# Second attention: the causal mask taken from TensorE products to a minimum on VectorE

## What is computed

```python
scores = jnp.einsum('bhqd,bhkd->bhqk', q, k) / jnp.sqrt(jnp.asarray(d_k, x.dtype))
causal = jnp.tril(jnp.ones((t, t), dtype=bool))
scores = jnp.where(causal, scores, jnp.asarray(-jnp.inf, scores.dtype))
attn = jax.nn.softmax(scores, axis=-1)
y = jnp.einsum('bhqk,bhkd->bhqd', attn, v)
```

## Time and profile before

| | us |
|---|---|
| three runs | 711.42, 712.61, 714.70 (median 712.61) |
| the profiled execution | 712.78 |
| its span, first to last instruction | 711.0 |
| PE busy | 636.5 (90%) |
| DVE busy | 450.6 (63%) |
| ACT busy | 324.3 (46%) |
| POOL busy | 120.9 (17%) |

### The profile page before, as it was taken

One profiled execution on the slowest core, in us unless ns is written; L12 is line 12 of the kernel. 1 busy time (PEld: TensorE's weight loads), 2 busy tenths in 40 slices (PEclk: granted clock), 3 DMA queues, 4 the chain that ended last, 5 costly groups with the idle time before them and its releaser, 6 DMA issues.

```text
span 711.0 us, 11162 instructions
## 1 busy us (share of the span) xinstructions
PE 636.5 (90%) x4151; PEld 393.0 (55%) x4204; DVE 450.6 (63%) x1270; ACT 324.3 (46%) x548; POOL 120.9 (17%) x117
## 2 busy tenths in 40 slices
PE   6877665576999999999999999999999999999897
PEld 2755223363567667666666666555565655554443
DVE  4687658426575775775775776765857576665364
ACT  2477456314555655655655655344433534352110
POOL 2130001132133133132122222011020200000000
PEclk9987987678999999999999999999999999999899
DMA  9300000299965974975894791909166290000000
GB/s 345 169 0 1 0 0 15 50 119 132 120 105 75 99 109 80 87 116 84 74 121 79 69 130 42 97 21 117 13 100 50 61 89 16 1 16 1 16 0 30
DMA packets 83261, 50.64 MB, mean 71 GB/s; under 512 B 4052, under 2 KB 82644, under 8 KB 82900
## 3 DMA queue, kind: packets, MB, share of 16 engines
q1 hardware_dynamic: 83208, 49.94, 48.4%
HBM read 35.11 MB, written 14.68 MB: 70 GB/s over the span
## 4 chain that ended last, share of the span: by engine, by line
PE 61%; DVE 10%; DMA 4%; issue 4%; ACT 2%; SPq 1%; POOL 1%; DVEq 0%; ACTq 0%
PE ps L1241 15%; PE ps L1123 11%; PE ps L1114 7%; PE ps L1187 4%; PE ps L1198 4%; PE ps L1183 4%; PE ps L1106 3%; PE ps L1158 3%; PE ps L1166 3%; PE ps L1212 2%; PE ps L1205 2%; DVE nmax L1395 2%; DMA KS<-parts_dram 2%; PE ps L1161 2%; DVE xn L1353 1%
## 5 line engine op out<-in xcount | busy, mean ns | idle before, releaser
L1395 DVE TENSOR_REDUCE nmax<-ps 128x2 f32<-128x512 f32 (+1 forms) x192 | 130.9, 687 | 82.2 <-PE ps L1166 49.9
L1290 ACT ACTIVATE PT<-ps 128x512 f32<-128x512 f32 x192 | 114.7, 599 | 110.3 <-PE ps L1187 108.2
L1241 PE MATMUL ps<-wm,xnT 128*128 128x512 f32 x256 | 121.2, 604 | 0.0
L1284 ACT ACTIVATE QS<-ps 8x1024 bf16<-8x1024 f32 x64 | 65.0, 1016 | 48.1 <-PE ps L1171 47.3
L1066 POOL TENSOR_TENSOR rstd<-ve,fix 128x2 f32<-128x2 f32 x32 | 22.3, 697 | 355.4 <-DVE ve L1348 355.4
L1187 PE MATMUL ps<-QS,KS 110*128 110x256 bf16 (+3 forms) x512 | 74.5, 247 | 0.0
L1474 DVE SCALAR_TENSOR_TENSOR acc<-ps,gate,acc 128x256 f32<-128x256 f32 x128 | 61.6, 481 | 19.5 <-PE ps L1241 17.0
L1114 PE MATMUL ps<-xnT,wt 128*128 128x256 f32 x256 | 66.5, 409 | 6.5 <-ACT xnT L1257 6.5
L1241 PEld LDWEIGHTS ps<-wm,xnT 128*128 128x128 f32 x256 | 45.5, 192 | 39.6 <-issue 39.1
L1086 POOL TENSOR_TENSOR parts<-rest,fix 128x512 bf16<-128x512 f32 x30 | 38.1, 1271 | 148.0 <-DVE rest L1366 105.5
L1183 PE MATMUL ps<-fixb 128*128 128x256 bf16 (+1 forms) x192 | 60.4, 314 | 1.7 <-DVE nmax L1395 0.3
(11 more groups left out here) (206 smaller groups left out, 922.1 us busy)
## 6 DMA issues: line engine op xcount, KB each, us to landing
parts_dram<-parts SPq DMA_DIRECT2D x32, 384.0 KB, 3.3
QS<-parts_dram SPq DMA_DIRECT2D x96, 128.0 KB
KS<-parts_dram SPq DMA_DIRECT2D x96, 128.0 KB, 9.4
wt<-wt_dram SPq DMA_DIRECT2D x1, 2562.0 KB, 18.5
wm<-wm_dram SPq DMA_DIRECT2D x1, 2449.0 KB, 12.9
xc<-x_dram SPq DMA_DIRECT2D x8, 256.0 KB, 5.3
out_dram<-res SPq DMA_DIRECT2D x8, 256.0 KB, 2.2
w<-w_dram SPq DMA_DIRECT2D x1, 845.0 KB, 7.5
```

Source lines behind the costliest of these rows:

```text
L1241: mm = pe.matmul(d, normT(stage, batch)[:, c, t * P:(t + 1) * P], M("We", c * EXPERTS * CH + e * 2 * CH, 2 * CH), start=(c == 0), stop=(c ...
L1284: act.activation(QS[MAX_AT:MAX_AT + MAX_ROWS, stack(stage, batch), 4 * n:4 * n + 4, :], bank(piece)[MAX_AT:MAX_AT + MAX_ROWS, 0:PIX].unsqu ...
L1290: act.activation(PT[:, n % PT_RING, :], bank(piece), ACT.Exp).then_inc(drain(piece), 1)
L1395: dve.tensor_reduce(group[:, 0, :] if part == 0 else group[:, 1, 2 * part - 2:2 * part], bank(piece).rearrange("p (j n) -> p j n", n=w_), ...
```

## The change

For stage 2 the mask product in front of X is left out, and the first score product starts the bank. A new piece Z comes on DVE for every X of stage 2, in the step after it: it takes the minimum of PT's diagonal blocks and a table `causal`, which holds 3e38 where the key may be seen and 0 where not. PT's blocks are 2 heads of 128 queries for parts 0 and 1 (256 columns) and 4 heads for part 2 (512 columns). Z waits for ACT's exponential, and O0 and O1 wait for Z. The table is made once by two DVE instructions in PAD, between its memsets and `chosen`.

```diff
-def attention():
+def attention(stage):
...
     out += [("X", u, u + LAG) for u in range(UNITS)]
+    if stage == 2:
+        out += [("Z", u, u + LAG + 1) for u in range(UNITS)]
     out += [("O0", g, 3 * g + LAG + 3) for g in range(GROUPS)]
...
-                    pe.matmul(d.rearrange("p (j n) -> p j n", n=width)[:, :, 0:P], FB("tri0", 0, P),
-                              FB("ident").unsqueeze(1).broadcast_to([P, len(heads), P]), start=True, stop=False,
-                              skip_group_check=True)
+                    if stage == 0:
+                        pe.matmul(d.rearrange("p (j n) -> p j n", n=width)[:, :, 0:P], FB("tri0", 0, P),
+                                  FB("ident").unsqueeze(1).broadcast_to([P, len(heads), P]), start=True, stop=False,
+                                  skip_group_check=True)
...
-                                       QS[r, at, 4 * g + j, kt * P:], start=False, stop=(k == len(heads) - 1),
+                                       QS[r, at, 4 * g + j, kt * P:], start=(stage == 2 and k == 0), stop=(k == len(heads) - 1),
...
+                    wait(pe, "causal", ("Z", stage, batch, 3 * n + 1))
...
+                    wait(pe, "causal", ("Z", stage, batch, 3 * n + 2))
...
+                    dve.wait_ge(fix_loaded, 16)
                     dve.wait_ge(fixb_loaded, 16)
+                    settle(dve.tensor_scalar(causal[:], FB("tri0", 0, P), 0.0, KEPT, ALU.is_lt, ALU.mult))
+                    settle(dve.scalar_tensor_tensor(causal[:], F("ident"), KEPT, causal[:], ALU.mult, ALU.add))
...
+                if kind == "Z":
+                    drained(dve, ("X", stage, batch, n))
+                    width = P if n % 3 == 2 else PIX
+                    diagonal = PT[:, n % PT_RING, :].rearrange("p (j n) -> p j n", n=width)[:, :, 0:P]
+                    dve.tensor_tensor(diagonal, diagonal, causal[:].unsqueeze(1).broadcast_to([P, 512 // width, P]),
+                                      ALU.min).then_inc(sems["causal"], 1)
```

More of the change, by code:

```diff
@@ L36 @@
 MASKED = -1e30
+KEPT = 3e38
 QUARTERS = (2, 0, 3, 1)
@@ L141, in in_order @@
     for at, (s, b) in enumerate(BODIES):
-        for k, (kind, n, step) in enumerate(attention()):
+        for k, (kind, n, step) in enumerate(attention(s)):
             group = 0 if engines == "tensor" or kind in ("S", "MS", "M") else 2
@@ L153 @@
 JOBS = ("S", "M", "X", "OX", "T", "Q", "K", "V", "AT", "PR", "FF", "R", "GT", "GB", "E", "CT")
-SETTLED = {"LNa": 2, "MS": 1, "OX": 1, "R": 1, "RT": 3, "E": 1}
+SETTLED = {"LNa": 2, "MS": 1, "OX": 1, "R": 1, "RT": 3, "E": 1, "PAD": 2}
 def settled(piece):
@@ L172, in signals @@
     out += {"LNa": [("var_ready", 1), ("rstd_ready", 1)], "LNb": [("xn_ready", 1)], "XB": [("x_biased", 1)],
-            "MS": [("max_split", 1)], "PAD": [("padded", 3), ("chosen", 1), ("chosen_spread", 16 * (STACKS - 1))], "CT": [("out_stored", 16)],
+            "MS": [("max_split", 1)], "Z": [("causal", 1)], "PAD": [("padded", 3), ("chosen", 1), ("chosen_spread", 16 * (STACKS - 1))], "CT": [("out_stored", 16)],
             "Q": [("first_ready0", 1)], "K": [("first_ready1", 1)],
@@ L950, in build @@
             chosen = lb("chosen", [P, HEADS // GROUPS], BF16)
+            causal = lb("causal", [P, P])
             oinv = lb("oinv", [P, 2, 2, 4])
```

## The result

| | before | after |
|---|---|---|
| median of the runs | 713.56 us (4 runs, 711.42 to 714.7) | 723.22 us (4 runs, 720.83 to 724.1) |
| ratio to before, 95% interval | | **1.0134** (1.0096 to 1.0172) |
| the profiled execution, its span | 712.78, 711.0 us | 724.1, 722.3 us |
| mean granted clock of PE | 0.950 | 0.933 |

What follows compares the result with a forecast made beforehand. PE was taken to bound windows 9 and 12, DVE parts of window 10. To 712.78 us came +3.3 for the queue and +2.4 for one clock fall: 718.5 profiled, 718.3 median, range 710.8 to 723.0.

Steps and rivals of the forecast that it cites:

- window 9: O0 of step 3 waits for the late minimum of step 2, partly offset by removed masks: net +1.3 us.
- window 10: Late minima on DVE delay T, O0 and the gates, less the masks saved behind GT: net +1.5 us.
- windows 11 to 13: Minima on DVE's full queue delay X of step 8, less later masks saved: +0.54 each, +1.6 us together.
- windows 14, 15: X of step 8 waits and PR waits for ACT, leaving a saving of 0.2 each, -0.4 us together.
- sum of the queue: All window terms and PAD added together, without PE's clock: +3.3 us.
- the clock: PE's idle in window 9 brings one fall to half clock, costing 0 to 3.0 us, taken as +2.4.
- Rival C: Clock falls in window 9 and window 10 or more: 720.7 us, up to 722; chance 0.17.
- G: Something slower that had not been seen, beyond 722 us; chance 0.04.
- B: The same DVE delays as forecast but no fall of PE's clock: 715.9 us; chance 0.20.
- E: PE bounds everywhere, minima never stand in front of what it needs: -9.3 us, 703.3 us; chance 0.04.
- D: The minimum is cheap on DVE's queue (0.30 and 0.17 us): -1.7 us, 710.9 us; chance 0.15.
- F: Neighbours set a product's share of PE, so a wide mask gives back only 0.13 us: 721.0 us; chance 0.03.

Runs made afterwards that it cites:

- again: The changed kernel itself, unaltered, run again: ratio 1.0169 to the kernel before, median 723.73 us.
- filler_masks: Changed kernel with unused scrap products filling PE's long waits in windows 9 and 10, and mask products back in windows 14 and 15: 715.10 us, ratio 1.0035.
- again_2: The changed kernel itself, unaltered, run a third time: 721.51 us in one run.
- early: The change for batches 0 to 2 only, batches 3 to 7 keeping their mask products: 720.36 us in one run.
- none: Changed kernel with neither mask products nor minima, so the second attention is not masked: 708.65 us in one run.
- slack: Changed kernel with minima only for units 0 to 4 of each batch and from unit 6 in batch 7, mask products elsewhere: 710.86 us, ratio 0.9972.
- trim: As slack, but mask products also kept in windows 14 and 15 (units 0 to 4 of batch 6): 708.58 us, ratio 0.9948.

## Why the prediction was wrong, step by step

| step | predicted | measured, without a fall or beside the same one |
|---|---|---|
| window 8 | -0.7 | -0.67 |
| window 9 | +1.3 | +1.31 |
| window 10 | +1.5 | +1.51 |
| windows 11 to 13 | +1.6 | +1.3 (0.44 each) |
| windows 14, 15 | -0.4 | -0.1 (36.18 in window 14) |
| window 16 | -0.6 | -0.7 (28.92 in again) |
| PAD | +0.6 | +0.4, the start of `chosen` 137.24 for 136.85 |
| sum of the queue | +3.3 | +3.1 by these, +2.5 (0.8 to 4.2) by the ratio of filler_masks |
| the clock | +2.4 | **+7 to +9.5** |

For window 16 the kernel before has 29.60 us with the first 2.0 us of its own fall in it. The like of it is again, whose fall begins 2.1 us ahead of the last PR; the -1.1 of the table above is against a window with 0.8 us of a fall.

**What held.** The direction, the mechanism and the place: PE waits for the minimum of step 2 at O0 of window 9 (2.11 or 2.12 us, in four profiles), T and GT of window 10 wait longer (2.18 and 1.02, for 1.21 and 0.57), the spacing of the minimum, and every queue term within 0.4. The idle of window 9 is split: X ahead of O0 waits 0.67 us for the late row maximum, and only the rest is the minimum's, so that O0's row shows 2.12 and not the 2.4 to 3 forecast. O0 comes 0.08 later than reckoned, because it starts 0.14 us behind the end of the minimum (394.17) where I had put 0.07. In window 10 O0 of step 6 waits the 2 us forecast in again and again_2 (2.1), but only 0.2 in the first profile, where PE was late by then from running at half clock. The start-up's +0.4 can't be seen in the whole: the first PR lay between 201.8 and 206.7 us in the 14 profiles, without regard to the kernel.

**The step that failed** is the term "one fall +2.4", by number and by length. Length: I took the 6 us that the earlier trace rows showed as the length of a fall; the same wait of window 9 (2.11 or 2.12 us) gave 10.2, 6.8, 3.4 us and nothing (after, early, again_2, again), and 10.2 us cost 4.42 in window 9, above my 3.0 for one. Where PE waits anyway, in window 10, 10.2 us cost 1.58 there and 0.77 in early. Number: I looked for falls only where the new waits are long, 2 and 3 us. The falls of windows 14 and 15 need no long wait. They come with PE's removed work, which had filled the time between waits of 0.2 to 0.5 us, and go when it is put back; I wrote -0.4 for those windows, a pure saving. By the medians an execution of the changed kernel has 26 to 30 us more at half clock than one before, about four falls of 6.8, for 7 to 9.5 us (the 9.5 to 12 of the two ratios less 2.5). At the 0.36 us of the kernel before for each us at half clock, 26 to 30 would come to 9.5 to 11, an estimate. Rival C (two or more falls, "720.7, up to 722") was nearest in mechanism, and had a chance of 0.17; by its time alone the result fell to G, the rest beyond 722, with 0.04.

**The rivals.** B had the right time for a kernel without falls (715.9; filler_masks 715.1), E the right size for the masks alone (none is 8.1 us shorter from the first PR on, for 9.3). D, the cheap minimum, is excluded by the spacing. F, a wide mask worth only 0.13 us, is not borne out (the Trainium skill, "TensorE: Matmul & The Clock Gate", section "Back-to-back issue gap", gives that figure for a sustained stream). The spacing of a wide mask is still 0.22 in slack (599.12 to 599.34) and in trim (602.58 to 602.80). And window 8, which loses four small masks and one wide one and waits for no minimum, is shorter by 0.67: less 4 x 0.115, that leaves 0.21 for the wide one.

**Still open**: why one wait of 2.12 us brings a fall in one execution and none in another. The place of the wait in time differs between them by up to 3 us with the start-up, and no run held that fixed.

## What to carry to other kernels

Work taken off the busiest engine was worth its spacing only where no wait lay next to it (window 8); near short waits it was worth nothing, and less than nothing where it had kept PE's clock up (windows 14 and 15). Before work moves to an engine with a lower average load, look for the step where that engine is *late*, not how busy it is: with the 50 minima of such steps back on PE slack turned +1.3% or more into -0.3%, and with 10 more in windows 14 and 15 trim made it -0.5%. And when an estimate depends on clock falls, price it as a distribution over executions, with the granted clock of all runs and not of the profiled one alone.

## What the runs showed that I had not expected

**A minimum beside POOL.** 84 of the 96 minima last 0.41 to 0.69 us. Twelve, two in each of windows 8 to 13, last longer, eleven of them 1.11 to 1.55. DVE and POOL in window 9, after:

```profile
411.40 1.38 DVE L1419 TENSOR_TENSOR PT<-PT,causal 128x512 f32<-128x512 f32 x1
...
414.73 1.12 DVE L1419 TENSOR_TENSOR PT<-PT,causal 128x256 f32<-128x256 f32 x1
```
```profile
410.97 1.27 POOL L1090 TENSOR_TENSOR parts<-rest,fix 128x512 bf16<-128x512 f32 x1 [12.47 <-DVE rest L1373]
412.32 1.49 POOL L1094 TENSOR_TENSOR parts<-rest,parts 128x512 bf16<-128x512 f32 x1
414.30 1.27 POOL L1090 TENSOR_TENSOR parts<-rest,fix 128x512 bf16<-128x512 f32 x1 [0.49 <-DVE rest L1373]
```

They lie beside POOL's two-input instructions, which split the operands, and both can grow: the minimum by 0.70, POOL's second instruction from 1.15 to 1.49. In every such pair of this profile it is the one that started later that grew: in windows 11 to 13 the wide minimum starts 0.16 us behind POOL's second instruction and lasts 1.54 to 1.55, and POOL's stays at 1.16. The mean by shape shows it too:

```profile
L1419 DVE TENSOR_TENSOR PT<-PT,causal 128x256 f32<-128x256 f32 x64 | 30.8, 482 | 0.0
L1419 DVE TENSOR_TENSOR PT<-PT,causal 128x512 f32<-128x512 f32 x32 | 25.9, 810 | 0.0
```

482 and 810 ns for the 420 and 690 that I had reckoned, 56.7 us together for 49. (DVE's busy time grew by only 47.1, since neighbours overlap.) It costs nothing here, since these steps come after a window's tight ones; filler_masks has them too and is at the sum. No run kept POOL away from them, so the cause is not shown beyond this coincidence.

**A clock fall at full work.** In the 9.70 us at half clock after window 9's wait PE was busy for 9.69. I had thought of a fall as short once work is back.
